# Gelu stages that scatter finished rows by their number instead of gathering them by slot, and a relu stage in one run of tiles

## The chip, the cores and the metric

The kernel runs on one core of a Trainium2 chip. The metric is the time on the device in microseconds (us); lower is better. The core's engines each follow a program of their own and meet at semaphores: TensorE (PE in the rows), VectorE (DVE), ScalarE (ACT), GpSimd (POOL) and SyncE (SP), which here only starts DMAs.

## The reference

2,048 tokens of 128 numbers go through six layers in float32:

```
x = x + 0.5 * FFN0(layernorm(x))   # stage a: 8 experts, gelu, top 2, width 512
x = x + attention(layernorm(x))    # b: 2 x 1,024 tokens, 16 heads, causal, rotated q and k
x = x + 0.5 * FFN0(layernorm(x))   # c: the same weights as a
x = x + 0.5 * FFN1(layernorm(x))   # d: 8 experts, relu, top 1, width 256
x = x + scan(layernorm(x))         # e: state-space scan
x = x + 0.5 * FFN1(layernorm(x))   # f: the same weights as d

FFN0: w, e = top_k(softmax(h @ Wr + br), 2)
      out  = sum over both: w * (gelu(h @ up[e].T) @ down[e].T)
FFN1: e    = argmax(h @ Wr + br), p its probability
      out  = p * (relu(h @ w1[e] + b1[e]) @ w2[e] + b2[e])
```

## The kernel before, in words

The tokens stay on chip in `x`, 16 tiles of 128 rows, as two blocks `b` of 8 tiles. A mixture sorts the rows of a block by expert, so that every tile of 128 sorted rows has one expert. In a gelu stage a block gives 16 row sets (8 tiles, two choices each) and at most NTG = 23 sorted tiles; in a relu stage 8 row sets and NTL = 15 tiles.

**A gelu stage** (a from 49.3 us, c from 570.3). For each block the tasks `stats`, `norm`, `turn` normalize and transpose the rows, `glogits`, `gpick`, `gcount`, `gslots` pick two experts and compute each row's slot (`gslot_of`). GpSimd then sends 16 indirect DMAs, each 128 rows of `xn` to the scratch memory `xs` (L1654, `gelu_scatter`); in stage a SyncE has cleared that memory with zeros first, and block 1's first scatter waits for it. SyncE loads the sorted rows to `gxt` in four pieces (GLOADS). Then come 46 tiles, block 0's and block 1's, as a software pipeline over 48 steps `s`: TensorE transposes tile s (L802), VectorE copies the expert's up weights (L1905; ScalarE does it from step HANDED = 34), TensorE multiplies tile s-1 (L811), ScalarE applies gelu to it (L1240), TensorE multiplies tile s-2 by the down weights (L820), and ScalarE copies the result into `gxt`. SyncE stores the finished tiles in four pieces to `ys`. When all four are there, GpSimd gathers them with 16 indirect DMAs of 128 rows (L1661, `gelu_gather`) to `gyg`, and the task `gadd` adds them to `x`, weight times row, in 16 operations on VectorE (L1835). The weights come from the task `gweights` at steps 16 and 17.

Between these, GpSimd also sends block 1's scatter (behind block 0's), in stage a a chain of small operations on the bias b2 (`bias_parts`, L1645) and the clearing of attention's padded areas (`clear_pads`). All in the order of its program: it has one queue, and so has SyncE.

**Other work beside the tiles.** Each engine holds a list `along` of tasks that it does behind its own part of a step. At HANDED, VectorE starts block 0's `gadd` and its normalization for the next stage, so that only block 1's remains for the next stage. In attention, block 1's tasks are called `second` and stand between the score blocks of the first unit: its `gadd` behind block 14.

**The first relu stage** (d, from 728 us). Block 0's slots are ready by then. Its tiles run in two runs: block 0's 15 (18 steps), then the list `between` (block 1's `gadd`, normalization, logits, slots), then block 1's scatter, load and tiles. A relu tile has a transpose (L863), up matmuls (L870), VectorE's copy (L1924), transposes back (L877), relu on ScalarE, down matmuls (L884, L886) and VectorE's copy of the result (L1934). Block 0's rows are stored, gathered and added in the second run. The last stage (f) has one run over both blocks already, and GpSimd writes each of its finished tiles to the output with one indirect DMA (L1711), rows by their token numbers, at the pace in which tiles end.

## Time and profile before

| | us |
|---|---|
| median of 3 runs | 1326.39 |
| lowest, highest | 1318.11, 1328.89 |
| profiled execution, device time | 1318.07 |
| its span in the trace | 1316.3 |

Shares of the span in which an engine is busy: PE 71%, DVE 54%, ACT 45%, POOL 45%. The mean granted clock of TensorE is 0.825 of full speed. In a row of windows stand the stretch, its length, the busy us and count of PE, PEld, DVE, ACT and POOL, the granted clock, the DMA share and GB/s. Every time in the rows counts from the start of the span. "Idle before" is the time for which an engine did nothing ahead of an instruction, and the name behind the arrow is what ended it; "remote" stands for a release that no instruction or DMA of the trace explains, "issue" for none at all.

### The profile page before, as it was taken

The page shows a single profiled execution, that of the slowest core. Times are in us where ns is not written, and L with a number is a line of the kernel's source. Part 1 is how long each engine was busy: PE and PEld are TensorE (multiplying, and loading weights), DVE is VectorE, ACT ScalarE, POOL GpSimd, SP SyncE. Part 2 cuts the span into 40 slices and gives each one's busy share as a digit, 9 for nine tenths or more (in the row PEclk, how much of TensorE's full clock was granted, in tenths as well). Part 3 has the DMA queues.
Part 4 walks back from the last instruction along what each step waited for, and adds up shares of the span by engine and source line. Part 5 has one row for each costly group of instructions (what it writes and reads, how often), then busy time and mean ns, then how long its engine had stood idle before and what let it go on. Part 6 is the DMA issues. An engine that isn't in the chain of part 4 may idle for free. (4 is left out here: it accounts for less than half of the span.)

```text
span 1316.3 us, 27353 instructions
## 1 busy us (share of the span) xinstructions
PE 940.3 (71%) x9756; PEld 616.6 (47%) x9756; DVE 714.2 (54%) x1903; ACT 595.3 (45%) x1264; POOL 586.3 (45%) x585
## 2 busy tenths in 40 slices
PE   2768763688888887775876655463788888886686
PEld 2668650212222223355765443223566666665464
DVE  4222247667778874322221152556578888886432
ACT  1224450246666667242454222256456566651243
POOL 2462325643333311414212427232468888883454
PEclk9969785669999998687979777786678999986688
DMA  6531112132211100031311211103311111101320
GB/s 221 159 98 47 33 46 49 32 93 63 63 33 33 31 3 1 22 121 49 95 30 47 73 37 55 43 4 132 80 34 38 39 39 40 39 24 65 117 87 16
DMA packets 113706, 76.72 MB, mean 58 GB/s; under 512 B 56768, under 2 KB 107980, under 8 KB 112616
## 3 DMA queue, kind: packets, MB, share of 16 engines
q1 hardware_dynamic: 106727, 61.32, 16.8%
q0 software_dynamic: 6848, 13.67, 3.4%
q8 instruction: 82, 1.34, 0.4%
q14 instruction: 49, 0.39, 0.1%
HBM read 41.98 MB, written 29.46 MB: 54 GB/s over the span
## 5 line engine op out<-in xcount | busy, mean ns | idle before, releaser
L1625 POOL TENSOR_TENSOR arena<-arena 128x512 f32<-128x512 f32 x126 | 215.0, 1725 | 86.6 <-ACT arena L1344 37.4
L1344 ACT ACTIVATE arena<-ps 128x512 f32<-128x512 f32 x256 | 143.4, 596 | 107.8 <-PE ps L1039 101.9
L1296 ACT ACTIVATE arena<-ps 128x1024 f32<-128x1024 f32 (+1 forms) x192 | 148.2, 810 | 86.8 <-PE ps L944 83.2
L2035 DVE TENSOR_TENSOR arena<-arena,ps 128x1024 f32<-128x1024 f32 x189 | 154.4, 857 | 18.7 <-PE ps L1052 17.7
L929 PE MATMUL ps<-arena 64*128 64x512 bf16 (+3 forms) x384 | 109.7, 363 | 57.0 <-DVE maxima L1963 20.8
L1963 DVE CUSTOM_DVE_ANT_0 arena<-ps,arena 128x512 f32<-128x512 f32 (+3 forms) x256 | 112.1, 488 | 46.8 <-PE ps L929 40.0
L811 PE MATMUL ps<-arena 128*128 128x128 f32 x736 | 106.6, 291 | 33.6 <-issue 21.4
L820 PE MATMUL ps<-arena 128*128 x736 | 106.0, 290 | 32.1 <-ACT arena L1240 20.1
L1549 POOL TENSOR_SCALAR_AFFINE_SELECT arena<-arena 128x512 f32<-128x512 f32 x64 | 41.1, 642 | 186.9 <-ACT arena L1296 186.4
L1905 DVE COPY arena<-arena 128x512 f32 x68 | 33.2, 489 | 163.1 <-PE ps L811 81.0
L811 PEld LDWEIGHTS ps<-arena 128*128 128x128 f32 x736 | 96.2, 204 | 39.9 <-issue 24.5
L1661 POOL DMA_INDIRECT arena<-ys_rows,gslot_of x64 | 61.4, 959 | 117.8 <-DMA ys_rows<-arena 99.3
L820 PEld LDWEIGHTS ps<-arena 128*128 128x128 f32 x736 | 96.3, 204 | 35.9 <-issue 35.7
L929 PEld LDWEIGHTS ps<-arena 64*128 64x128 bf16 x384 | 28.2, 95 | 179.6 <-DVE maxima L1963 90.0
L1654 POOL DMA_INDIRECT xs_rows<-xn,gslot_of x64 | 62.1, 971 | 90.0 <-DVE gslot_of L1822 57.6
L959 PE MATMUL ps<-arena 128*32 128x512 f32 (+3 forms) x768 | 89.0, 538 | 7.4 <-POOL arena L1549 7.4
L1966 DVE TENSOR_REDUCE maxima<-ps 128x1 f32<-128x512 f32 x128 | 81.0, 684 | 21.9 <-PE ps L929 20.5
L2047 DVE TENSOR_TENSOR arena<-arena 128x1024 f32<-128x1024 f32 x63 | 77.6, 1232 | 26.9 <-ACT arena L1344 26.9
L1067 PE MATMUL ps<-arena 128*32 128x128 f32 x2048 | 86.2, 321 | 0.1
L944 PE MATMUL ps<-arena 64*128 64x512 bf16 (+3 forms) x384 | 83.0, 352 | 4.4 <-ACT arena L1296 4.4
L1240 ACT ACTIVATE arena<-ps 128x512 f32<-128x512 f32 x92 | 55.2, 600 | 67.2 <-PE ps L811 35.2
L1052 PE MATMUL ps<-arena 12*128 12x128 bf16 x1024 | 56.6, 237 | 16.9 <-DVE arena L2035 14.1
(245 smaller groups left out, 1672.1 us busy)
## 6 DMA issues: line engine op xcount, KB each, us to landing
ys_rows<-arena SPq DMA_DIRECT2D x8, 512.0 KB, 3.5
xw_rows<-blank_dram SPq DMA_DIRECT2D x2, 1935.0 KB, 8.9
arena<-xs_rows SPq DMA_DIRECT2D x6, 512.0 KB
arena<-xw_rows SPq DMA_DIRECT2D x2, 1032.0 KB
xs_rows<-arena SPq DMA_DIRECT2D x4, 512.0 KB, 7.0
arena<-up_dram SPq DMA_DIRECT2D x4, 512.0 KB, 7.1
arena<-dn_dram SPq DMA_DIRECT2D x4, 512.0 KB, 7.8
arena<-up_dram SPq DMA_DIRECT2D x2, 1024.0 KB, 6.3
```

The lines of the kernel that those rows point to most:

```text
L811: mm = e.matmul(ps[:, n1 % 2, c * P:(c + 1) * P], gwup[:, n1 % 2, c * P:(c + 1) * P], gxT[:, n1 % 2, :], start=True, stop=True)
L820: mm = e.matmul(ps[:, 4 + n2 % 2, 0:P], ghT[:, n2 % 2, c * P:(c + 1) * P], wdn[:, bass.ds(ex, 1), c, :].rearrange("p e d -> p (e d)"), sta ...
L929: mm = e.matmul(ps[:, n % 2, m * w:(m + 1) * w], qT[vp][rows, i, h // HP, :], kT[v % 3][rows, 4 * half:4 * half + w // P, h // HP, :], sta ...
L944: mm = e.matmul(ps[:, 2 + 2 * pair + h, 0:w], kT[v % 3][rows, j, pair, :], qm[rows, vp, pair, half * 512 + q0:half * 512 + 512], start=Tru ...
L959: mm = e.matmul(ps[32 * h:32 * h + 32, 6 + half, q0:512], vpad[:, vp, j, h, :], probT[:, n % 2, h, 0:w], start=(j == 0), stop=(w == P), sk ...
L1067: mm = e.matmul(ps[32 * ml:32 * ml + 32, 6 + u % 2, 0:D], cz[:, u % 2, ml, (4 * mh + t4) * 32:(4 * mh + t4 + 1) * 32], hsf[t % 3][:, m * D ...
L1296: e.activation(probT[:, m % 2, 2 * pair:2 * pair + 2, 0:w], ps[:, 2 + 2 * pair:4 + 2 * pair, 0:w], ACT.Exp, scale=SCALE).then_inc(AT["exp_ ...
L1344: e.activation(to, ps[:, 4 + n % 2, :].rearrange("p (d m t) -> p t m d", d=DBK, t=TU), ACT.Exp, scale=-1.0).then_inc(SC["decay_ready"], 1)
L1625: e.tensor_tensor(hsf[t % 3][:, cols], decayf[u % 2][:, t4 * W + cols.start:t4 * W + cols.stop], hsf[(t - 1) % 3][:, cols], ALU.mult).then ...
L1963: ins = e.tensor_tensor_reduce(masked_s[n % 2][:, m * w:(m + 1) * w], of, causal[:, 4 * P - w:4 * P], 1.0, MASKED, ALU.add, ALU.max, to)
L1966: ins = e.tensor_reduce(to, of, AX.X, ALU.max)
L2035: e.tensor_tensor(to, to, of, ALU.add).then_inc(SC["added"], 1)
```

## The change

Scattering by row number in place of the gathers. The sorted row now has GRW = 130 numbers: 128 of data, its weight and the number of its place in the block's result, 2 x 1,024 rows. Both are put in ahead of the scatter, so `gweights` moves in front of `gcount` and `gslots`. The source of the scatter is a new area `gsrc` with one copy of the rows for each choice; ScalarE makes the second. The scatter's targets are cleared with a table `gblank` from memory whose rows carry a number out of bounds, which the later DMA drops. When a tile is finished, ScalarE copies it times its weight (a column of the tile), and GpSimd sends that tile at once, by the numbers in its rows, to `yk`. When all 23 of a block have landed, SyncE loads the result with one DMA to `gyg`, and `gadd` is two additions over 128x1024.

One run in the relu stage. `between` is gone; block 1's tasks hang on steps 0 to 7 of the tiles of block 0. GpSimd sends block 0's relu scatter behind tile AHEAD = 14 of the last gelu block. HANDED falls to 30, and in attention block 1's tasks start behind score block 3.

The core of the diff:

```diff
+GRW = D + 2
+AHEAD = 14
...
-HANDED = 34
+HANDED = 30
...
+        gsrc = [[at(a0, TOP * HT * GRW).rearrange("p (k i r) -> p k i r", k=TOP, r=GRW) for a0 in pair]
+                for pair in ((10240, 12320), (SIDE0, 6144))]
...
-        GROUTED = ["glogits", "gpick", "gcount", "gslots"]
+        GROUTED = ["glogits", "gpick", "gweights", "gcount", "gslots"]
...
-            scalar[16], vector[17] = weights, weights
...
-                between = [(gelus[1], "gadd", 1)] + rows_of(st, 1) + [t(w, 1) for w in ROUTED]
-                runs = ((0, NTL), (NTL, B * NTL))
-                along = {5: [t("rweights", 0)], NTL + 5: [t("rweights", 1)]}
+                along = {"vector": {0: [(gelus[1], "gadd", 1), t("stats", 2)], 1: [t("norm", 2), t("stats", 3)], 2: [t("norm", 3)],
+                                    5: [t("rpick", 1)], 7: [t("rslots", 1)]},
+                         "tensor": {2: [t("turn", 2)], 3: [t("turn", 3)], 4: [t("rlogits", 1)], 6: [t("rcount", 1)]},
+                         "scalar": {0: [t("stats", 2)], 2: [t("turn", 2), t("stats", 3)], 3: [t("turn", 3)]}}[engine]
+                along.update({9: [t("rweights", 0)], NTL + 5: [t("rweights", 1)]})
...
-            second = {14: (0, 1), 18: (2,), 19: (3, 4), 23: (5,), 24: (6,), 27: (7,)}
+            second = {3: (0, 1), 7: (2,), 8: (3, 4), 12: (5,), 13: (6,), 16: (7,)}
...
+            def clear(m, b):
+                sp.dma_start(scratch[f"xg{m}{b}"], t_in["gblank"]).then_inc(rows_clear[b], 16)
...
-            def gelu_put(m, b, stores):
-                for i0, i1 in stores:
-                    sp.wait_ge(GT["y_copied"], (B * m + b) * NTG + i1)
-                    sp.dma_start(scratch[f"ys{b}"][i0 * P:i1 * P, :].rearrange("(i p) d -> p i d", p=P), gxt[b][:, i0:i1, :]
-                                 ).then_inc(gys_in[b], 16)
-
+            def gelu_rows(m, b):
+                sp.wait_ge(gput[b], 16 * NTG * (m + 1))
+                sp.dma_start(gyg[b].rearrange("p k i d -> p (k i) d"),
+                             scratch[f"yk{b}"].rearrange("(n p) d -> p n d", p=P)).then_inc(ys_in[b], 16)
...
-                    put(0, STORES)
+                    put(0, STORES[:2])
                     fetch(1)
+                    put(0, STORES[2:])
...
+            elif what == "norm" and st["kind"] == 0:
+                b, tiles = g * TPB // HT, slice(g * TPB % HT, g * TPB % HT + TPB)
+                rows = gsrc[st["ghalf"] // B][b]
+                e.wait_ge(LN["xn_ready"], st["norm"] + g + 1)
+                e.copy(rows[:, 1, tiles, 0:D], rows[:, 0, tiles, 0:D]).then_inc(GT["rows_copied"], 1)
...
-                    e.copy(gxt[b][:, i, :], ps[:, 4 + n2 % 2, 0:P]).then_inc(GT["y_copied"], 1)
+                    row = gxt[b][:, i]
+                    e.activation(row[:, 0:D], ps[:, 4 + n2 % 2, 0:P], ACT.Copy, scale=row[:, D:D + 1]).then_inc(GT["y_copied"], 1)
...
             def gelu_scatter(m, b):
-                if m == 0:
-                    e.wait_ge(rows_clear[b], CLEAR)
+                e.wait_ge(rows_clear[b], CLEAR[m])
                 e.wait_ge(GT["slots_ready"], B * m + b + 1)
                 for k in range(TOP):
+                    if k == 1:
+                        e.wait_ge(GT["rows_copied"], NTB // B * (B * m + b + 1))
                     for i in range(HT):
-                        e.indirect_dma_start(scratch[f"xs{b}"], bass.IndirectOffsetOnAxis(ap=gslot_of[:, b, k, i:i + 1], axis=0),
-                                             xn[:, b * HT + i, :], None).then_inc(grows_moved[b], 16)
-
-            def gelu_gather(m, b):
-                e.wait_ge(gys_in[b], 16 * len(GSTORES) * (m + 1))
-                for k in range(TOP):
-                    for i in range(HT):
-                        e.indirect_dma_start(gyg[b][:, k, i, :], None, scratch[f"ys{b}"],
-                                             bass.IndirectOffsetOnAxis(ap=gslot_of[:, b, k, i:i + 1], axis=0)).then_inc(grows_moved[b], 16)
+                        e.indirect_dma_start(scratch[f"xg{m}{b}"], bass.IndirectOffsetOnAxis(ap=gslot_of[:, b, k, i:i + 1], axis=0),
+                                             gsrc[m][b][:, k, i, :], None).then_inc(grows_moved[b], 16)
+
+            def gelu_rows_out(m, b):
+                for i in range(NTG):
+                    if (m, b, i) == (1, 1, AHEAD):
+                        relu_scatter(relus[0], 0)
+                    row = gxt[b][:, i]
+                    e.wait_ge(GT["y_copied"], (B * m + b) * NTG + i + 1)
+                    e.indirect_dma_start(scratch[f"yk{b}"], bass.IndirectOffsetOnAxis(ap=row[:, D + 1:GRW].bitcast(U32), axis=0),
+                                         row[:, 0:D], None, bounds_check=TOP * S - 1, oob_is_err=False).then_inc(gput[b], 16)
...
-                gelu_gather(m, 0)
+                gelu_rows_out(m, 0)
                 if m == 0:
                     clear_pads()
-                    gelu_gather(0, 1)
+                gelu_rows_out(m, 1)
...
-                relu_scatter(st, 0)
-                if st is relus[0]:
-                    gelu_gather(1, 1)
-                    relu_gather(0, 0)
+                if st is relus[-1]:
+                    relu_scatter(st, 0)
                 relu_scatter(st, 1)
                 if st is relus[0]:
+                    relu_gather(0, 0)
...
+                    e.tensor_copy(rows.rearrange("p k i r -> p (k i) r")[:, :, D + 1:GRW].bitcast(I32), token_of[:].unsqueeze(2))
                     link(e.reciprocal(w[:, 0], w[:, 0]))
-                    link(e.tensor_scalar(w[:, 0], w[:, 0], 0.5, None, ALU.mult))
-                    link(e.tensor_tensor(w[:, 1], w[:, 0], gshift[:, g, :, E], ALU.mult))
+                    link(e.tensor_scalar(rows[:, 0, :, D], w[:, 0], 0.5, None, ALU.mult))
+                    link(e.tensor_tensor(rows[:, 1, :, D], rows[:, 0, :, D], gshift[:, g, :, E], ALU.mult))
                 elif what == "gadd":
-                    e.wait_ge(grows_moved[g], GMOVE * (2 * m + 2))
+                    e.wait_ge(ys_in[g], 16 * (m + 1))
+                    xs = x[:, g * HT:(g + 1) * HT, :]
                     for k in range(TOP):
-                        for i in range(HT):
-                            xs = x[:, g * HT + i, :]
-                            e.scalar_tensor_tensor(out=xs, in0=gyg[g][:, k, i, :], scalar=gweight[:, g, k, i:i + 1], in1=xs,
-                                                   op0=ALU.mult, op1=ALU.add).then_inc(GT["added"], 1)
-                        e.wait_ge(GT["added"], (q * TOP + k + 1) * HT)
+                        e.tensor_tensor(xs, xs, gyg[g][:, k], ALU.add).then_inc(GT["added"], 1)
+                        e.wait_ge(GT["added"], q * TOP + k + 1)
```

**GpSimd, from block 0's scatter of the second gelu stage to the end of the relu stage.** `xs`, `xg` are sorted rows, `ys`, `yk` results, the digit behind is the block (`xg10` is stage c, block 0). Before:

```order
L1654 DMA xs0_rows<-xn,gslot_of 2944x128 x16
L1654 DMA xs1_rows<-xn,gslot_of 2944x128 x16
L1661 DMA arena<-ys0_rows,gslot_of 128x128 x16
L1683 DMA xs0_rows<-xn,slot_of 2944x128 x8
L1661 DMA arena<-ys1_rows,gslot_of 128x128 x16
L1689 DMA arena<-ys0_rows,slot_of 128x128 x8
L1683 DMA xs1_rows<-xn,slot_of 2944x128 x8
L1701 MEMSET arena 128x4096
L1701 MEMSET arena 128x16384
L1689 DMA arena<-ys1_rows,slot_of 128x128 x8
```

Now:

```order
L1658 DMA xg10_rows<-arena,gslot_of 2944x130 x16
L1658 DMA xg11_rows<-arena,gslot_of 2944x130 x16
L1667 DMA yk0_rows<-arena 2048x128 x23
L1667 DMA yk1_rows<-arena 2048x128 x14
L1689 DMA xs0_rows<-xn,slot_of 1920x128 x8
L1667 DMA yk1_rows<-arena 2048x128 x9
L1689 DMA xs1_rows<-xn,slot_of 1920x128 x8
L1695 DMA arena<-ys0_rows,slot_of 128x128 x8
L1706 MEMSET arena 128x4096
L1706 MEMSET arena 128x16384
L1695 DMA arena<-ys1_rows,slot_of 128x128 x8
```

The two bursts of 16 gathers are gone and 46 scatters of finished tiles stand there, split behind the 14th of block 1; block 1's relu scatter is ahead of block 0's gather.

**VectorE, where block 1's rows enter the first relu stage.** Before, with the last three result copies of block 0's tiles ahead:

```order
L1934 COPY arena<-ps 128x128 x3
L1835 SCALAR_TENSOR_TENSOR x<-arena,gweight,x 128x128 x16
L1748 BN_STATS stats<-x 128x6 x4
L1753 BN_AGGR mv<-stats 128x2 x4
L1764 RECIPROCAL rstd<-std 128x4
L1771 TENSOR_SCALAR xn<-x,mv,rstd 128x128 x4
```

Now, with the first copies of block 0's tiles (L1924) between:

```order
L1863 CAST slot_of<-best8 128x8
L1839 TENSOR_TENSOR x<-x,arena 128x1024 x2
L1752 BN_STATS stats<-x 128x6 x4
L1757 BN_AGGR mv<-stats 128x2 x4
L1924 COPY arena<-ps 128x256
L1768 RECIPROCAL rstd<-std 128x4
L1775 TENSOR_SCALAR xn<-x,mv,rstd 128x128 x4
```

The 16 additions are two, and the norm of block 1 stands among the copies of block 0's first tiles instead of behind its last.

## Rows read from the trace of the kernel before

**Rows 1.** Windows of three stages.

```profile
49.30:186.00 136.70, 105.16 (x805) 98.97 (x804) 32.06 (x94) 63.77 (x163) 46.77 (x45) 0.86 0.28 79
570.30:710.60 140.30, 105.86 (x850) 100.36 (x848) 37.00 (x140) 70.61 (x171) 30.64 (x32) 0.88 0.21 66
728.00:837.70 109.70, 68.35 (x345) 47.80 (x342) 36.31 (x127) 33.39 (x100) 43.42 (x30) 0.77 0.16 46
```

**Rows 2.** Transposes L802 in five stretches: durations in ns, first and last start.

```profile
L802 PE MATMUL ps<-ident,arena x9: 272/273/273, 105.1 to 120.4; 128*128 128x128 f32 x9
L802 PE MATMUL ps<-ident,arena x5: 272/272/421, 122.3 to 146.8; 128*128 128x128 f32 x5
L802 PE MATMUL ps<-ident,arena x5: 273/273/421, 601.3 to 625.3; 128*128 128x128 f32 x5
L802 PE MATMUL ps<-ident,arena x4: 272/272/421, 648.0 to 670.5; 128*128 128x128 f32 x4
L802 PE MATMUL ps<-ident,arena x5: 272/401/421, 61.4 to 88.2; 128*128 128x128 f32 x5
```

**Rows 3.** Timelines of POOL and DVE, first gelu stage: start, duration, [idle before].

```profile
59.29 0.95 POOL L1654 DMA_INDIRECT xs_rows<-xn,gslot_of  x1 [13.95 <-DMA xs_rows<-arena]
120.36 1.02 POOL L1661 DMA_INDIRECT arena<-ys_rows,gslot_of  x1 [28.98 <-DMA ys_rows<-arena]
139.19 0.94 POOL L1661 DMA_INDIRECT arena<-ys_rows,gslot_of  x1 [0.31 <-issue]
121.74 0.43 DVE L1905 COPY arena<-arena 128x512 f32 x1 [1.47 <-PE ps L811]
```

**Rows 4.** Timeline of ACT, first gelu stage, same columns.

```profile
137.36 0.60 ACT L1240 ACTIVATE arena<-ps 128x512 f32<-128x512 f32 x1 [6.61 <-remote]
```

**Rows 5.** GpSimd's DMAs to the output, last stage (by line).

```profile
L1711 POOL DMA_INDIRECT out_dram<-arena x25: 981/982/993, 1255.7 to 1299.5; - x25
```

**Rows 6.** Timeline of DVE, last stage.

```profile
1254.50 0.35 DVE L1931 SCALAR_TENSOR_TENSOR arena<-ps,arena 128x128 f32<-128x128 f32 x1 [4.59 <-remote]
```

**Rows 7.** Timelines of DVE and POOL, first gelu stage.

```profile
82.08 3.00 DVE L1905 COPY arena<-arena 128x512 f32 x2 [12.23 <-remote]
101.78 0.22 DVE L1826 TENSOR_REDUCE gweight<-gshift 128x8 f32<-128x64 f32 x1 [2.22 <-ACT gshift L1207]
90.27 1.11 POOL L1645 CAST b2p<-arena 3x1024 bf16<-3x1024 f32 x1
```

**Rows 8.** Timelines of PE, DVE, POOL and ACT, opening of attention.

```profile
203.99 0.40 PE L929 MATMUL ps<-arena 64*128 64x128 bf16 x4 [16.96 <-issue]
217.29 4.41 DVE L1835 SCALAR_TENSOR_TENSOR x<-arena,gweight,x 128x128 f32<-128x128 f32 x16
243.38 4.49 POOL L1584 TENSOR_TENSOR arena<-arena,bqkv 128x2048 f32<-128x2048 f32 x1 [11.56 <-ACT arena L1317]
266.08 1.51 ACT L1296 ACTIVATE arena<-ps 128x768 f32<-128x768 f32 x2 [1.60 <-POOLq L1517]
268.42 1.94 PE L959 MATMUL ps<-arena 128*32 128x512 f32 x8 [2.95 <-POOL arena L1549]
```

**Rows 9.** The page, costliest groups and DMA issues (KB each, us to landing).

```profile
L2047 DVE TENSOR_TENSOR arena<-arena 128x1024 f32<-128x1024 f32 x63 | 77.6, 1232 | 26.9 <-ACT arena L1344 26.9
arena<-up_dram SPq DMA_DIRECT2D x2, 1024.0 KB, 6.3
```

**Rows 10.** Timelines of DVE, POOL and PE, first relu stage.

```profile
743.45 0.29 DVE L1934 COPY arena<-ps 128x128 f32<-128x128 f32 x1 [10.82 <-remote]
770.03 3.09 DVE L1835 SCALAR_TENSOR_TENSOR x<-arena,gweight,x 128x128 f32<-128x128 f32 x11
791.64 1.00 POOL L1683 DMA_INDIRECT xs_rows<-xn,slot_of  x1 [9.63 <-DVE slot_of L1860]
804.96 0.45 PE L863 MATMUL ps<-ident,arena 128*128 128x128 f32 x1 [13.13 <-issue]
```

**Rows 11.** Transposes L863 of the relu stage's second run (by line).

```profile
L863 PE MATMUL ps<-ident,arena x15: 272/273/472, 805.0 to 831.0; 128*128 128x128 f32 x15
```

More of the change, by code:

```diff
@@ L346, in gelu_tasks @@
             tensor, scalar, vector = {}, {}, {}
-            weights = [t("gweights", b) for b in range(B)]
             if st is gelus[0]:
@@ L379, in relu_tasks @@
                 before = [k for b in range(B) for k in rows_of(st, b) + [t(w, b) for w in ROUTED + ["rweights"]]]
-                between = []
-                runs = ((0, B * NTL),)
                 along = {}
-            return before, between, runs, along
+            return before, ((0, B * NTL),), along
         AT = {k: sem(f"att_{k}") for k in (
@@ L509, in _ @@
             sp.dma_start(before_f, t_in["before"]).then_inc(route_in, 16)
[L511 to L514 removed]
+            sp.dma_start(token_of[:], t_in["tokens"]).then_inc(route_in, 16)
+            def clear(m, b):
+                sp.dma_start(scratch[f"xg{m}{b}"], t_in["gblank"]).then_inc(rows_clear[b], 16)
             sp.dma_start(x[:, HT:NT, :], x_dram[:, HT:NT, :]).then_inc(x_in, 16)
[L517 to L518 removed]
+            clear(0, 0)
             for ex in range(0, E, 2):
@@ L561, in _ @@
                     sp.dma_start(scratch[f"xw{v - 3}"], t_in["blank"]).then_inc(rows_clear[v - 3], 16)
+                if v in (1, 2):
+                    clear(1, v - 1)
+                if v in (5, 6):
+                    sp.dma_start(scratch[f"xs{v - 5}"], t_in["blank"][0:NTL * P, 0:D]).then_inc(rows_clear[v - 5], 16)
                 sp.wait_ge(AT["unit_split"], 2 * v + 2)
@@ L692, in n_tile @@
                 return xw[:, i, 0:D]
+            if st["kind"] == 0:
+                return gsrc[st["ghalf"] // B][i // HT][:, 0, i % HT, 0:D]
             i0 = xn_at(st, i // TPB) + i % TPB * P
@@ L827, in relu_mixture_tensor @@
             nf = F1 // P
-            before, between, runs, along = relu_tasks(st, nxt)
+            before, runs, along = relu_tasks(st, nxt, "tensor")
             def keep(n):
@@ L843, in relu_mixture_tensor @@
             for first, last in runs:
-                if first > 0:
-                    for task in between:
-                        task_tensor(e, *task)
                 for s in range(first, last + 3):
@@ L855, in relu_mixture_tensor @@
                                 e.wait_ge(rows_moved[b], MOVE * (2 * m + 1))
-                            if st is relus[0]:
-                                keep(KEEP[1 + b])
+                            if st is relus[0] and b == 0:
+                                keep(KEEP[1])
                             e.wait_ge(RT["slots_ready"], st["half"] + b + 1)
@@ L1250, in relu_mixture_scalar @@
             nf = F1 // P
-            before, between, runs, along = relu_tasks(st, nxt)
+            before, runs, along = relu_tasks(st, nxt, "scalar")
             for task in before:
@@ L1254, in relu_mixture_scalar @@
             for first, last in runs:
-                if first > 0:
-                    for task in between:
-                        task_scalar(e, *task)
                 for s in range(first, last + 3):
@@ L1910, in relu_mixture_vector @@
             def relu_mixture_vector(e, st, nxt):
-                before, between, runs, along = relu_tasks(st, nxt)
+                before, runs, along = relu_tasks(st, nxt, "vector")
                 for task in before:
@@ L1914, in relu_mixture_vector @@
                 for first, last in runs:
-                    if first > 0:
-                        for task in between:
-                            task_vector(*task)
                     for s in range(first, last + 3):
@@ L2144, in constants @@
                                  np.full((NTL * P, 1), NOWHERE, np.int32).view(np.float32)], axis=1),
+        "gblank": np.concatenate([np.zeros((NTG * P, GRW - 1), np.float32),
+                                  np.full((NTG * P, 1), NOWHERE, np.int32).view(np.float32)], axis=1),
         "before": (n[:, None] < n[None, :]).astype(np.float32),
```

90 lines of the change are left out of this document (41 added, 49 removed).

## The prediction

> **What bounds the kernel now.** I read the windows by stage first, then the engines' timelines inside the four windows that the change touches. The chain of waits covers only the end, so it doesn't help here. In the gelu stages (49.3 to 186 and 570.3 to 710.6) no engine is full: TensorE's matmul records cover 105 of 137 us, its granted clock is 0.86 and 0.88 [rows 1]. Two paces explain that. Undisturbed, nine transposes L802, one a tile, start from 105.1 to 120.4: 15.3/8 = 1.91 us a tile. In four other places five starts, or four in the third, take 24.5, 24.0, 22.5 and 26.8 us, 6 to 7.5 a tile; the lowest are 6.1 and 6.0 [rows 2]. Each of the four lies on a burst in which GpSimd issues 16 indirect DMAs, one row set every (139.19-120.36)/15 = 1.26 us; the slow tiles go on until some 3 us after the last [rows 3]. What is late there is a signal: ScalarE stands for 6.61 us in which TensorE's matmuls were long over, with "remote" as releaser [rows 4]. So **a burst of indirect DMAs beside the tile pipeline costs its length plus 3 us, less the tiles that crawl through**.
>
> The counter-example matters most. In the last stage GpSimd issues one indirect DMA for each finished tile, 25 from 1255.7 to 1299.5, 43.8/24 = 1.83 us apart, and there the tiles run at pace [rows 5]: only the burst ahead of them left a 4.59 us remote wait at 1254.50 [rows 6]. The change turns the gelu gathers into that pattern. Its success depends on whether GpSimd is at pace, or behind and so in a burst.
>
> **The change, part by part.** The sums are against the profiled execution, 1318.07 us (span 1316.3), which is at the low end of the runs shown (1318.11 to 1328.89, median 1326.39).
>
> Opening. The weights now come ahead of the slots: five small VectorE operations of 0.22 us [rows 7], so +1.1 us in front of the first scatter. ScalarE's copy of the rows for the second choice lies beside TensorE's transposes: nothing, and 0.6 us for each at worst if that cover were gone. The blank rows are now copied from memory; they are issued where zeros went out before and have over 20 us: nothing. Rows of 520 instead of 512 bytes: nothing.
>
> First gelu stage (a). Block 1's scatter no longer waits for its clearing, which is issued earlier, so its burst moves from 59.29 to some 49, just when the tiles start. Before, it cost 26.8-4x1.91 = 19.2 us [rows 2, 3]. After: slow from 50.5 to 72, 21.5 us with 3.5 tiles, costs 14.8; behind it the eight chained operations on b2, which run to 91.4 before, lengthen weight copies (3.00 us for two) [rows 7] and cost perhaps 2.5. Term -1.9. The gather of block 0 goes: 24.5-7.6 = -16.9. The weights' stop at tile 16 goes (8x0.22 = 1.8 us of VectorE [rows 7], behind ScalarE's exponential, which I put at as much again with the restart): -3.
>
> Added: the y scatters. GpSimd reaches the first only after its b2 work, at some 82, with 9 tiles finished. It sends one every 1.26 us (0.796 a us), the crawling pipeline adds one every 6.1 (0.164), so the backlog drains in 9/0.63 = 14 us. With the 3 us behind it that is 17 us for 2.8 tiles: +12. From there on it's one scatter a tile, 1.26 in 1.91 us, and I take nothing: the bounds are 0 [rows 5] and the full crawl of 4.2 us a tile [rows 2]; I take the near end since the form is the same (one tile, rows of 512 bytes, indices beside them, out-of-bounds rows dropped). clear_pads between the blocks lets 3 tiles pile up: +3. Stage a: 1.1-1.9-16.9-3+12+3 = **-6**.
>
> Here a rule speaks against the change. VectorE's weight copy (0.43 us, 128x512 fp32, SBUF to SBUF) runs every tile; one of GpSimd's gathers was under way when the copy at 121.74 ran, another stood alone at 139.19, and the step stayed 1.26 us over all 16 [rows 3]. The Trainium skill (SBUF — State Buffer, "Who interferes with whom") says that such a copy locks GpSimd out of the shared port, so that its descriptors wait. By the rows the sum has no term; by the rule each scatter would be longer, which is rival 4.
>
> Attention's opening (186 to 268.4). It starts with an idle TensorE until 203.99, behind the two transposing DMAs and beside the second gather burst. Then come 16 additions of 4.41 us at 217.29, which now are two over 128x1024 each (such an operation takes 1.23 on average in another stage [rows 9]); and GpSimd's rotation from 243.38 on, for which ScalarE waits 1.60 us at 266.08 and TensorE 2.95 us at 268.42 [rows 8]. The gathers are gone (-4, a choice: their 3 us tail and some delay of the transposes), additions -2, and because block 1's tasks move from score block 14 to 3, the rotation starts earlier and the last two waits go, -4.5. Late next: block 1's y rows, landed and read back (1 MB takes 6.3 us [rows 9], so 1.3+3+6.3+1 = some 12 us after the last tile), while the score blocks start 15 to 18 us after it: covered by little, so I give 2.5 back. Term **-8**. SP's two clears ahead of transposes 1 and 2 have tens of us.
>
> Second gelu stage (c). The second gather goes: four starts from 648.0 to 670.5 are three steps, 22.5-3x1.91 = -16.8 [rows 2]. But block 1's scatter (601 to 620) stays, and GpSimd comes out of it with 15 finished tiles waiting: 15/0.63 = 24 us more of burst, in which 3.9 tiles pass: +16.4. Two copies and an earlier table change on ScalarE: +1.5. AHEAD: GpSimd stops at y tile 14 of block 1 for the relu slots (TensorE's count is at step 41), then sends 8 scatters and the 9 last tiles, 17x1.26 = 21 us of burst over the last 5 tiles, of which some two crawl fully: +9. The weights' stop -1. In return the relu stage starts sooner: 17.4 us lie between the last tile and 728 [rows 1]; after, the last y scatter, 3 us to land, SP's y load, then the tile load, 10.5 in all: -7. Sum -16.8+16.4+1.5+9-1-7 = **+2**.
>
> First relu stage (728 to 837.7). Now one run. Before: two runs with a seam: after the first, additions, norm, logits and slots up to 791.64, 8 scatters, tiles again at 804.96 [rows 10]. A tile takes (831.0-805.0)/14 = 1.86 us [rows 11], so 33 steps, the 30 tiles and 3 to fill and drain the pipeline, take 61.4. Block 1's scatter and block 0's gather become two bursts of 8 inside the run. At 743.45 a long burst ended in a remote wait of 10.82 [rows 10]; that of 8 in the last stage ended in one of 4.59 [rows 6], which with its restart I put at 6: 6 each. The routing tasks of block 1 sit between tiles; they fill VectorE's idle time where a tile leaves some, and hold the tiles where they wait in a chain: +8, between 0 and the 35 us that the seam takes (770.03 to 804.96). 61.4+12+8 = 81.4 against 109.7: -28. GpSimd's two memsets for the scan now end only about when the last y is stored: +2, a choice. Term **-26**.
>
> Sum: -6-8+2-26 = -38: 1318-38 = **1280 us**. The other runs shown lie up to 11 us above the profiled one, which I keep for the range.
>
> **The rivals.** (1) The y scatters don't crawl even when GpSimd is behind: rows 5 show a pace of 1.83, not 1.26, so nothing excludes it; against it, all four bursts did. Then 12+3+16.4+9 of the sum's costs go: **1240**. (2) Slower: even at one a tile they delay TensorE's signals. Place: steady gelu tiles, some 78 of 92; price 1.2 us a tile (0.6 on each of the two signals to ScalarE); -38+94 = +56, **1374**. It decides from 38/78 = 0.5 us a tile. For: a gelu tile has 17 matmuls where the last stage has 10, so more signals. Against: 25 in a row at pace [rows 5]. (3) The relu run buys little: VectorE in order stands through additions, norm and slots while the tiles wait, the tasks cost the whole 35 us instead of 8: 1280+27 = **1307**. (4) The lock: each scatter waits for a weight copy of 0.43, 1.69 us instead of 1.26; 9 tiles then drain in 9/(0.592-0.164) = 21 us and 15 in 35: +5 and +8 after the crawling tiles, and no room in the end phase, +4: **1297**; the rows of 0.95 us beside such copies speak against it.
>
> **How the numbers follow.** Forecast 0.55 (its own range 1262 to 1300), rival 1 0.18, rival 2 0.12, rival 3 0.10, rival 4 0.05. A change under 1% (13 us) can't be told from none. Faster: 0.53+0.18+0.05+0.03 = 0.79; same 0.02+0.05+0.02 = 0.09; slower 0.12. The range takes half of rival 1, which is at its lower end, and rival 3 with the 8 us by which the median lies above the profiled run: 1240 to 1315.
>
> **What would show it.** GpSimd's gather lines are gone and 92 scatters of y rows stand there, back to back from 82 to 96 and from 620 to 644, else one a tile; TensorE's transposes at 6 us in those stretches and at 1.9 outside. Stage a ends near 180, attention's first weighted sum starts near 254, relu's tiles start near 716 and end near 797. I'm wrong if the single scatters sit beside steps of over 2.4 us, if the 1.26 us bursts sit beside 1.9 us steps, if attention waits for the y rows, or if relu's first steps take over 5 us each.

## The result and the profile after

The changed kernel takes 1280.84 us (median of 4 runs, 1277.08 to 1286.18), the kernel before 1322.25 beside it; the ratio is 0.9696, 95% interval 0.9616 to 0.9776. The profiled execution took 1277.80 us, against 1318.07 before: 40.3 us less. The forecast was 1280.

From the page, the group of the y scatters (line, out<-in, count, busy us, mean ns, idle before and its releaser).

```profile
L1667 POOL DMA_INDIRECT yk_rows<-arena x92 | 91.5, 994 | 91.0 <-ACT arena L1250 75.1
```

Stage windows, with the columns of [rows 1]: stage a, stage c, the relu stage.

```profile
49.70:177.70 128.00, 101.40 (x807) 96.00 (x805) 39.99 (x95) 67.76 (x164) 76.39 (x74) 0.91 0.26 68
548.60:705.40 156.80, 103.94 (x850) 98.85 (x849) 34.37 (x125) 77.86 (x176) 67.51 (x69) 0.85 0.19 59
714.90:795.20 80.30, 61.49 (x333) 44.82 (x333) 32.45 (x115) 31.94 (x99) 32.51 (x18) 0.89 0.19 56
```

| from, to | before | after | difference | forecast |
|---|---|---|---|---|
| start to first tile of a | 49.3 | 49.7 | +0.4 | +1.1 |
| stage a, to its last down matmul | 136.2 | 126.9 | -9.3 | -7.1 |
| to the first weighted sum | 82.9 | 71.7 | -11.2 | -8 |
| attention, to the first tile of c | 301.9 | 300.3 | -1.6 | 0 |
| stage c, to its last down matmul | 139.7 | 155.7 | +16.0 | +9 |
| to the first relu tile | 18.0 | 10.6 | -7.4 | -7 |
| relu stage, to its last down matmul | 109.2 | 79.2 | -30.0 | -28 |
| the rest | 479.1 | 481.9 | +2.8 | +2 |

The marks are first starts of the transposes and of the weighted sums and last starts of the down matmuls in the two traces. The differences add up to -40.3. Stage c, whose gathers were taken away, is 16 us longer than before.

**What a burst does.** Transposes of the gelu tiles by stretches, as in [rows 2]:

```profile
L804 PE MATMUL ps<-ident,arena x5: 272/273/327, 49.7 to 56.0; 128*128 128x128 f32 x5
L804 PE MATMUL ps<-ident,arena x16: 272/273/273, 97.8 to 126.3; 128*128 128x128 f32 x16
```

GpSimd beside them (a timeline's start and duration; then groups by line with first and last start):

```profile
49.27 0.96 POOL L1658 DMA_INDIRECT xg_rows<-arena,gslot_of  x1 [3.58 <-DVE gslot_of L1826]
68.31 0.96 POOL L1658 DMA_INDIRECT xg_rows<-arena,gslot_of  x1 [0.30 <-issue]
L1667 POOL DMA_INDIRECT yk_rows<-arena x8: 982/984/1040, 82.2 to 91.3; - x8
L1667 POOL DMA_INDIRECT yk_rows<-arena x13: 982/982/984, 99.2 to 121.9; - x13
```

While the single y scatters follow the tiles, 12 steps of 1.89 us from 99.2 to 121.9, the tiles are at pace: 15 steps of 1.90. Beside block 1's scatter, 16 in (68.31-49.27)/15 = 1.27 us each, the first five tiles are at pace too, and then no transpose starts from 56.04 to 74.74. The trace before has the same: beside its burst from 59.29 on, transposes start at 61.35 and 63.25, at pace, and then at 71.87, 84.58 and 88.21. Over the whole stretch that looked like a slow crawl; it is tiles at pace, then a stop. The stop in the timelines of PE, ACT, SyncE and DVE (SPq is a DMA issue, here the loads that wait for the 16 scatters):

```profile
54.14 0.27 PE L804 MATMUL ps<-ident,arena 128*128 128x128 f32 x1
54.25 1.06 PE L813 MATMUL ps<-arena 128*128 128x128 f32 x8
56.04 0.27 PE L804 MATMUL ps<-ident,arena 128*128 128x128 f32 x1
61.52 0.37 ACT L1250 ACTIVATE arena<-ps,arena 128x128 f32<-128x128 f32 x1 [7.28 <-remote]
63.63 0.27 ACT L1230 COPY arena<-ps 128x128 f32<-128x128 f32 x1 [1.75 <-remote]
63.95 2.08 PE L813 MATMUL ps<-arena 128*128 128x128 f32 x8 [7.64 <-issue]
70.61 2.11 SPq L529 DMA_DIRECT2D arena<-xg_rows  x4
72.13 0.60 ACT L1244 ACTIVATE arena<-ps 128x512 f32<-128x512 f32 x1 [8.23 <-remote]
72.25 2.92 DVE L1908 COPY arena<-arena 128x512 f32 x2 [17.90 <-remote]
74.74 0.42 PE L804 MATMUL ps<-ident,arena 128*128 128x128 f32 x1
```

Counted in program order, the instructions pair up like this. The transpose of 54.14 is over at 54.41, and ScalarE's copy of it (L1230) starts at 63.63, 9.2 us later. The up matmuls of 54.25 are over at 55.31, and ScalarE's gelu (L1244) and VectorE's next weight copy, both of which wait for them, start at 72.13 and 72.25, 16.8 us later. In the other direction nothing is late: L1230 ends at 63.90, and TensorE's next up matmuls, which wait for it, start at 63.95. So it is TensorE's signals that arrive late, 9 us and then 17.

In stage c the backlog of 12 finished tiles joins the burst. Two stops stand there, until 598 and 619, as these rows of DVE and POOL show:

```profile
598.13 0.43 DVE L1908 COPY arena<-arena 128x512 f32 x1 [14.43 <-remote]
619.29 0.43 DVE L1908 COPY arena<-arena 128x512 f32 x1 [20.73 <-remote]
L1667 POOL DMA_INDIRECT yk_rows<-arena x12: 982/984/1027, 598.4 to 612.6; - x12
```

At the end of stage c the relu scatter of block 0 and seven finished tiles are a burst of 15 DMAs. The down matmuls that L1250 waits for at 695.53 are over at 684.68, the up matmuls that L1244 waits for at 701.86 at 687.25:

```profile
L1689 POOL DMA_INDIRECT xs_rows<-xn,slot_of x8: 955/959/962, 680.5 to 689.3; - x8
L1667 POOL DMA_INDIRECT yk_rows<-arena x7: 982/984/997, 690.6 to 698.3; - x7
695.53 0.37 ACT L1250 ACTIVATE arena<-ps,arena 128x128 f32<-128x128 f32 x1 [5.82 <-remote]
701.86 0.60 ACT L1244 ACTIVATE arena<-ps 128x512 f32<-128x512 f32 x1 [5.96 <-remote]
```

**Attention's opening** (against [rows 8]): TensorE starts at 191.26 instead of 203.99, the additions take 2.48 us instead of 4.41, the rotation starts at 219.71 instead of 243.38, and there is no wait in front of the first weighted sum.

```profile
191.26 0.40 PE L928 MATMUL ps<-arena 64*128 64x128 bf16 x4 [14.42 <-DMA arena<-arena]
248.33 1.93 PE L958 MATMUL ps<-arena 128*32 128x512 f32 x8
193.65 2.48 DVE L1839 TENSOR_TENSOR x<-x,arena 128x1024 f32<-128x1024 f32 x2
219.71 4.52 POOL L1586 TENSOR_TENSOR arena<-arena,bqkv 128x2048 f32<-128x2048 f32 x1 [13.45 <-ACT arena L1319]
```

**The relu stage** (against [rows 10, 11]): the first 12 steps, with block 1's tasks in them, take 29.1 us where 22.3 would be pace (1.86 a step); each burst of 8 stops the tiles once, 8.7 us and 11.7 us for two steps that take 3.7.

```profile
L862 PE MATMUL ps<-ident,arena x13: 272/273/446, 714.9 to 743.9; 128*128 128x128 f32 x13
L862 PE MATMUL ps<-ident,arena x3: 273/273/421, 743.9 to 752.6; 128*128 128x128 f32 x3
L862 PE MATMUL ps<-ident,arena x3: 272/421/421, 767.5 to 779.2; 128*128 128x128 f32 x3
L1689 POOL DMA_INDIRECT xs_rows<-xn,slot_of x8: 955/959/965, 738.8 to 747.6; - x8
L1695 POOL DMA_INDIRECT arena<-ys_rows,slot_of x8: 940/944/995, 763.1 to 771.9; - x8
```

### The profile page after: what moved, and what is told of

It is laid out like the page before. It is cut to its first block and busy times, and to the rows that moved or that the text cites. A ratio compares the mean times of both kernels' runs of the same rounds, so it can differ in the third digit from the quotient of the medians.

```text
span 1276.0 us, 27407 instructions
## 1 busy us (share of the span) xinstructions
PE 925.0 (72%) x9746; PEld 611.4 (48%) x9746; DVE 706.6 (55%) x1843; ACT 612.4 (48%) x1280; POOL 615.5 (48%) x612
## 5 line engine op out<-in xcount | busy, mean ns | idle before, releaser
L2035 DVE TENSOR_TENSOR arena<-arena,ps 128x1024 f32<-128x1024 f32 x189 | 154.9, 857 | 22.4 <-PE ps L1051 21.3
L928 PE MATMUL ps<-arena 64*128 64x512 bf16 (+3 forms) x384 | 107.6, 353 | 49.4 <-DVE maxima L1963 19.9
L1667 POOL DMA_INDIRECT yk_rows<-arena x92 | 91.5, 994 | 91.0 <-ACT arena L1250 75.1
L813 PE MATMUL ps<-arena 128*128 128x128 f32 x736 | 103.6, 286 | 40.3 <-ACT arena L1230 26.0
L822 PE MATMUL ps<-arena 128*128 x736 | 103.3, 286 | 37.8 <-ACT arena L1244 29.6
L813 PEld LDWEIGHTS ps<-arena 128*128 128x128 f32 x736 | 94.0, 200 | 45.5 <-ACT arena L1230 28.4
L822 PEld LDWEIGHTS ps<-arena 128*128 128x128 f32 x736 | 93.8, 200 | 40.8 <-issue 40.6
L1658 POOL DMA_INDIRECT xg_rows<-arena,gslot_of x64 | 62.5, 976 | 81.8 <-DVE gslot_of L1826 63.3
L943 PE MATMUL ps<-arena 64*128 64x512 bf16 (+3 forms) x384 | 80.3, 341 | 6.3 <-ACT arena L1298 6.3
L1244 ACT ACTIVATE arena<-ps 128x512 f32<-128x512 f32 x92 | 55.0, 598 | 58.5 <-remote 33.2
```

The costliest lines, as they stand in the source:

```text
L813: mm = e.matmul(ps[:, n1 % 2, c * P:(c + 1) * P], gwup[:, n1 % 2, c * P:(c + 1) * P], gxT[:, n1 % 2, :], start=True, stop=True)
L822: mm = e.matmul(ps[:, 4 + n2 % 2, 0:P], ghT[:, n2 % 2, c * P:(c + 1) * P], wdn[:, bass.ds(ex, 1), c, :].rearrange("p e d -> p (e d)"), sta ...
L928: mm = e.matmul(ps[:, n % 2, m * w:(m + 1) * w], qT[vp][rows, i, h // HP, :], kT[v % 3][rows, 4 * half:4 * half + w // P, h // HP, :], sta ...
L1667: e.indirect_dma_start(scratch[f"yk{b}"], bass.IndirectOffsetOnAxis(ap=row[:, D + 1:GRW].bitcast(U32), axis=0), row[:, 0:D], None, bounds_ ...
L2035: e.tensor_tensor(to, to, of, ALU.add).then_inc(SC["added"], 1)
```

## The experiments

The kernels ran in four jobs, each on a chip of its own, with the kernel before beside them: 1321.63, 1324.96, 1321.03 and, in the last, 1239.01 us. In the first three the kernel before takes what it took beside the changed kernel, so their times can be set against 1280.84 within a few us; the last stands apart and has its own paragraph.

**The relu stage in two runs again** (x1_two_runs):

```diff
-                along = {"vector": {0: [(gelus[1], "gadd", 1), t("stats", 2)], ...
+                between = [(gelus[1], "gadd", 1)] + rows_of(st, 1) + [t(w, 1) for w in ROUTED]
+                runs = ((0, NTL), (NTL, B * NTL))
...
-                    put(0, STORES[:2])
-                    fetch(1)
-                    put(0, STORES[2:])
+                    put(0, STORES)
+                    fetch(1)
...
+                    relu_gather(0, 0)
                 relu_scatter(st, 1)
```

> The changed kernel with its first relu stage in two runs again; the gelu stages are as changed. By the prediction's term the one run is worth 26 us, so 1281+26 = 1307 us. By rival 3 (the tasks of block 1 cost in the run what they cost at the seam) nothing or a few us: 1281 to 1286.

Measured: 1299.07 us, ratio 0.9827 (0.9800 to 0.9854). The one run is worth 18 us, not 26. Its transposes, by line:

```profile
L864 PE MATMUL ps<-ident,arena x30: 272/273/476, 721.8 to 813.0; 128*128 128x128 f32 x30
```

The stage takes 97.5 us from here to its last down matmul (819.3), against 79.2 with one run and 109.2 before. So 12 of the 30 us that this stage gained come from the rest of the change. Two reasons offer themselves, which no run separates: block 1's 16 gathers no longer stand beside its first run (the wait of 10.82 in [rows 10]), and the additions at the seam are two. Rival 3 falls.

**A rest between the indirect DMAs of block 1's scatter** (x2_spaced):

```diff
+            def rest(e):
+                pauses[0] += 1
+                e.memset(pause[:], 0.0).then_inc(paused, 1)
+                e.wait_ge(paused, pauses[0])
...
                                              gsrc[m][b][:, k, i, :], None).then_inc(grows_moved[b], 16)
+                        if b == 1:
+                            rest(e)
```

> After each indirect DMA of block 1's scatter in both gelu stages GpSimd clears 128x512 unused numbers (some 0.6 us), so they come some 1.9 us apart instead of 1.26. Theory A (a queue: TensorE's signals wait behind indirect DMAs that come faster than they are worked off): the stop of TensorE between 56.04 and 74.74 goes, its transposes stand 1.9 us apart beside these DMAs. Theory B (any indirect DMA issued beside the tiles holds up TensorE's signals, so a longer stretch of them costs more): the stop becomes 10 us longer. GpSimd comes to the finished tiles 10 us later by both, so the halts behind it grow: by A 1270 to 1285 us, by B 1295 to 1305.

Measured: 1285.22 us, ratio 0.9711 (0.9673 to 0.9749). Transposes and indirect DMAs, by line:

```profile
L807 PE MATMUL ps<-ident,arena x25: 272/273/273, 51.7 to 95.7; 128*128 128x128 f32 x25
L1666 POOL DMA_INDIRECT xg_rows<-arena,gslot_of x16: 953/963/966, 49.5 to 77.8; - x16
L807 PE MATMUL ps<-ident,arena x3: 273/421/421, 97.9 to 127.8; 128*128 128x128 f32 x3
L1677 POOL DMA_INDIRECT yk_rows<-arena x23: 982/983/1062, 92.5 to 121.0; - x23
```

With 1.89 us between the DMAs ((77.8-49.5)/15) 25 transposes stand 44.0/24 = 1.83 us apart: no stop. Theory A holds, and B falls. GpSimd then finds some 20 finished tiles and sends 23 back to back, and there the stop returns, 29.9 us for two steps: what the rests saved is lost there. A stop needs DMAs that come close together, and enough of them.

**How close, and what the new order waits for** (x5_all_spaced: the rest over 128x128 instead of 128x512, and `rest(e)` behind the y scatters as well):

> The changed kernel with a smaller rest (128x128 unused numbers cleared, some 0.3 us) behind each indirect DMA of block 1's scatter and behind each y scatter, so none of these come closer than some 1.55 us. Theory A (queue): if an indirect DMA is worked off within 1.5 us the halts of TensorE at 56 to 75, 87 to 95 and 585 to 622 go and the time falls to 1235 to 1250 us. If it takes longer, the halts come later in a stretch and last longer: 1275 to 1290. Theory B (any indirect DMA beside the tiles delays signals): the stretches of indirect DMAs are a quarter longer, 1285 to 1300.

Measured: 1287.19 us, ratio 0.9722 (0.9691 to 0.9753). Rows of PE, POOL and DVE:

```profile
L807 PE MATMUL ps<-ident,arena x8: 272/272/421, 56.1 to 78.1; 128*128 128x128 f32 x8
L1666 POOL DMA_INDIRECT xg_rows<-arena,gslot_of x16: 957/967/1042, 50.0 to 72.7; - x16
139.82 2.54 DVE L1850 TENSOR_TENSOR x<-x,arena 128x1024 f32<-128x1024 f32 x2 [27.63 <-DMA arena<-yk_rows]
```

At (72.7-50.0)/15 = 1.51 us a DMA seven steps take 22.0 us where 13.3 are pace, so 8.7 are lost, against 17.7 in the changed kernel (56.04 to 77.50 for two steps). The limit is thus between 1.5 and 1.9 us for one indirect DMA. Stage a as a whole gains nothing (127.4 us to its last down matmul, 126.9 in the changed kernel), and a new wait is why: the rest makes a y scatter take 2.0 us, more than a tile, GpSimd falls behind, and VectorE at step 30 stands 27.63 us for the rows of block 0; its norm is due at TensorE's step 36, whose transposes stop from 125.69 to 149.60.

**Bytes or rows.** x7_half_bytes sends half of each row, x9_half_rows half of the rows; in both, block 1's result is read from block 0's area, so their output is not the layer's:

```diff
# x7_half_bytes, block 1
-                        e.indirect_dma_start(scratch[f"xg{m}{b}"], ..., gsrc[m][b][:, k, i, :], None)
+                        e.indirect_dma_start(scratch[f"xg{m}{b}"].rearrange("n (h d) -> (n h) d", h=2), ..., gsrc[m][b][:, k, i, 0:GRW // 2], None)
# x9_half_rows, block 1
+                        half = slice(0, P // 2)
+                        e.indirect_dma_start(scratch[f"xg{m}{b}"], ... gslot_of[half, b, k, i:i + 1] ..., gsrc[m][b][half, k, i, :], None)
```

> Block 1's scatters in both gelu stages move 65 of a row's 130 numbers, for the same 128 rows (block 1's result is left out, and its y scatters drop rows). Theory A1 (the queue works off bytes): half the bytes, no halt between 56 and 75. Theory A2 (it works off rows or descriptors, whatever their size): the halt stays at some 17 us.

> Block 1's scatters in both gelu stages move 64 of the 128 rows of a tile, whole rows, still in 16 DMAs (half of block 1's rows are left out). With half the bytes per row the halt stayed at 18.5 us. Theory A2 (what is worked off slowly is a row or its descriptor): half the rows, the halt between 57 and 75 goes or is under 5 us. Theory A3 (it is the indirect DMA as such, whatever is in it): the halt stays at 16 to 19 us.

Measured, one run each: 1279.24 and 1280.63 us. The two transposes around the stop, of x7_half_bytes and then of x9_half_rows:

```profile
L804 PE MATMUL ps<-ident,arena x2: 273/347/421, 57.0 to 75.5; 128*128 128x128 f32 x2
```

```profile
L804 PE MATMUL ps<-ident,arena x2: 273/347/421, 57.8 to 75.7; 128*128 128x128 f32 x2
```

The stop is 18.5 and 17.9 us, against 18.7. Neither half the bytes nor half the rows shortens it. What is left is A3, the indirect DMA as such: how many there are and how close they come (1.27 us in x7_half_bytes, 1.20 in x9_half_rows).

**Block 0's relu scatter behind the last finished tile** (x4_no_ahead):

```diff
-                    if (m, b, i) == (1, 1, AHEAD):
-                        relu_scatter(relus[0], 0)
...
-                if st is relus[-1]:
-                    relu_scatter(st, 0)
+                relu_scatter(st, 0)
                 relu_scatter(st, 1)
```

> Block 0's relu scatter stands behind the last finished tile again instead of behind tile 14 of block 1. By the prediction's terms the halts at the end of stage c go (-9) and the relu stage starts later (+7): 1279. By the trace of the changed kernel the last tiles lose some 16 us beside that burst: the last down matmul ends near 690 instead of 704.7, the relu tiles start some 16 us behind it, near 707 instead of 714.9, 1273. Rival: the y scatters and the relu stage's beginning are late by the same, 1281.

Measured: 1273.41 us, ratio 0.9648 (0.9616 to 0.9681), 7 us better than the changed kernel by the medians. The intervals of the two ratios overlap, so the places in the traces have to show it.

```profile
L804 PE MATMUL ps<-ident,arena x46: 272/273/421, 551.5 to 685.6; 128*128 128x128 f32 x46
L862 PE MATMUL ps<-ident,arena x30: 272/273/421, 710.9 to 783.1; 128*128 128x128 f32 x30
```

The last down matmul of stage c starts at 690.3, 4.7 us behind the last transpose; in the changed kernel 21.7 lie between them (682.6 to 704.3). So AHEAD costs 17 us there and gives back 10 (20.6 instead of 10.6 from that matmul to the first relu tile): +7, which agrees with the medians, where the prediction had +9-7 = +2.

**The chain on b2 in the opening** (x8_b2_first, on top of x4_no_ahead; and x6_spaced_b2, which adds the rests of x5; SyncE's load of b2 moves up as well in both):

```diff
                 if m == 0:
+                    bias_parts()
                     gelu_scatter(0, 0)
                 gelu_scatter(m, 1)
-                if m == 0:
-                    bias_parts()
```

> x4_no_ahead with the chain on b2 in the opening, no rests. GpSimd reaches the finished tiles at 70 us instead of 82, in the halt, with 4 to 5 waiting instead of 9: the halt of 87 to 95 goes into the first, and the weight copies of 2.92 us beside the chain are 0.43. The prediction's terms for the backlog (12, at 9 tiles) and the chain (2.5) give 1273-8 = 1265. Rival: the backlog only joins the burst and lengthens the first halt by as much, 1273.

> As x5_all_spaced, with two more edits: GpSimd does the chain on b2 in the opening, where it is idle from 0.9 to 25.6, and block 0's relu scatter stands behind the last finished tile. Where 1.55 us is far enough: 7 us from the end of stage c (as x4_no_ahead) and some 5 us from stage a, so 1225 to 1240. Where it is not: 1262 to 1275.

Measured: 1273.99 us (ratio 0.9603, 0.9572 to 0.9634) and 1271.03 us (0.9579, 0.9535 to 0.9624). x8_b2_first misses its 1265: its median is that of x4_no_ahead, and its ratio is lower by 6 us' worth with intervals that overlap. VectorE's second group of normalizations and GpSimd's first scatter in it:

```profile
10.63 5.52 DVE L1772 TENSOR_SCALAR arena<-x,mv,rstd 128x128 f32<-128x128 f32 x4
30.30 1.16 POOL L1659 DMA_INDIRECT xg_rows<-arena,gslot_of  x1 [9.00 <-DVE gslot_of L1823]
```

The chain runs from 9.55 to 21.3 and the first scatter starts at 30.30; in x4_no_ahead it starts at 25.95, and the first tile at 51.2 instead of 54.5. Stage a itself is 3 us shorter (120.0 against 123.2 from first to last transpose), and the opening is 3 us longer. The traces show where: the four operations of L1772, which take 1.12 us in x4_no_ahead (from 10.67), take 5.52 beside the chain, and VectorE's last slots, for which GpSimd waits, are written at 29.22 instead of 24.86. So it is VectorE that GpSimd's chain delays. x6 has x5's wait for block 0's rows in it as well.

**Finished tiles before block 1's scatter in stage c** (x10_rows_first, on top of x4_no_ahead; x11_first_ahead is the same with AHEAD in place):

```diff
+                if m == 1:
+                    gelu_rows_out(m, 0, 0, FIRST)      # FIRST = 10
                 gelu_scatter(m, 1)
...
-                gelu_rows_out(m, 0)
+                gelu_rows_out(m, 0, FIRST * m)
```

> x4_no_ahead with GpSimd sending the first 10 finished tiles of stage c as they come, ahead of block 1's scatter, for whose slots it otherwise stands idle until 581. If the second halt of that stage (603.7 to 624.8 in x4_no_ahead) is the backlog of finished tiles joined to the burst of 16, it goes and the first one stays: 1273-19 = 1254 us. Rival: the halt depends only on how long GpSimd has work beside the tiles, the y scatters later in the stage stall TensorE instead: 1268 to 1273.

> x10_rows_first with AHEAD = 14 in place again (block 0's relu scatter behind tile 14 of block 1). If its loss in the changed kernel came from the backlog, here, with GpSimd at pace before it, only a burst of 8 is left: no difference to x10_rows_first within 5 us, or a gain of some 5. If it came from the burst itself beside the last tiles: 7 us slower than x10_rows_first, as the changed kernel is against x4_no_ahead.

Measured: x10_rows_first 1256.16 us, ratio 0.9528 (0.9470 to 0.9585), and x11_first_ahead 1267.47, ratio 0.9583 (0.9531 to 0.9635). x10_rows_first:

```profile
584.25 0.27 PE L805 MATMUL ps<-ident,arena 128*128 128x128 f32 x1
592.98 0.42 PE L805 MATMUL ps<-ident,arena 128*128 128x128 f32 x1
609.88 0.42 PE L805 MATMUL ps<-ident,arena 128*128 128x128 f32 x1
L805 PE MATMUL ps<-ident,arena x46: 272/273/421, 548.4 to 673.1; 128*128 128x128 f32 x46
L863 PE MATMUL ps<-ident,arena x30: 272/273/421, 698.0 to 767.1; 128*128 128x128 f32 x30
```

Stage c takes 124.7 us from first to last transpose, against 134.1 in x4_no_ahead: the two stops are 8.7 and 16.9 us (584.25 to 592.98 to 609.88) where x4_no_ahead has 16.6 and 21.1. The time is near the 1254 expected, but not in the way that was expected: the second stop did not go, both got shorter, and they gave 9 us of the 17. The rest of the difference lies in stretches that the edit leaves alone (3.1 us ahead of stage c, 3.1 in the relu stage) and can't be put down to it. This is the best version on chips with the same time before, 25 us below the changed kernel. With AHEAD in place x11_first_ahead is 11 us slower, on the same chip: from the first tile of c to the first of the relu stage it loses 5.7 us (155.3 against 149.6), near the 7 expected, and the rest again elsewhere. So it is the burst itself beside the last tiles, not the backlog ahead of it.

**Block 1's tasks in attention behind score block 14 again** (x3_second14):

```diff
-            second = {3: (0, 1), 7: (2,), 8: (3, 4), 12: (5,), 13: (6,), 16: (7,)}
+            second = {14: (0, 1), 18: (2,), 19: (3, 4), 23: (5,), 24: (6,), 27: (7,)}
```

> Only the tasks of block 1 in attention's opening start behind score block 14 again instead of 3. By the prediction the two waits of 1.60 and 2.95 us in front of the first weighted sum come back, 4.5 us less the 2.5 that an earlier wait for block 1's rows may cost now: 1281+2 to 1281+4.5. Rival: GpSimd's rotation is late either way, no difference.

Measured: 1289.0 us, ratio 0.9749 (0.9722 to 0.9776): 8 us slower, though only part of that is the edit's. From the last down matmul of stage a (181.9) to the first weighted sum (257.1) it takes 75.2 us, against 71.7 in the changed kernel and 70.9 in x1_two_runs, which has the opening unchanged: 3.5 to 4.3 us. Stage a itself, which the edit doesn't touch, is 5 us longer here, as in x1_two_runs (131.9 and 131.3 against 126.9): its stops differ by as much from run to run.

**The rest in stage c, on another chip** (x12_first_rest: x10_rows_first with the rest of x5 behind block 1's scatter in stage c alone):

```diff
+                        if (m, b) == (1, 1):
+                            rest(e)
```

> x10_rows_first with the rest of x5_all_spaced (128x128 unused numbers) behind each indirect DMA of block 1's scatter in stage c alone, so these come some 1.47 us apart. The two halts there (584 to 593 and 593 to 610 in x10_rows_first, 22 us lost) shrink to the 5 us that this distance cost in x5_all_spaced; but the tiles then finish beside it, some 12 wait when GpSimd comes to them, and their burst costs some 12 us (8 waiting cost 5 to 7 in stage a): 1256-22+5+12 = 1251 us. Rival: GpSimd, not the halts, sets the end of the stage, as it has its 4 us more of work: 1256 to 1260.

Measured: 1209.85 us, against 1239.01 before on that chip, ratio 0.9742 (0.9707 to 0.9776). The rows of stage a, which this kernel has as x4_no_ahead has it: transposes, block 1's scatter, y scatters; then a transpose of stage c.

```profile
L808 PE MATMUL ps<-ident,arena x33: 272/273/273, 57.5 to 118.2; 128*128 128x128 f32 x33
L1667 POOL DMA_INDIRECT xg_rows<-arena,gslot_of x16: 957/962/1163, 46.3 to 65.5; - x16
L1676 POOL DMA_INDIRECT yk_rows<-arena x23: 984/984/1234, 80.6 to 109.2; - x23
590.14 0.45 PE L808 MATMUL ps<-ident,arena 128*128 128x128 f32 x1 [9.53 <-issue]
```

The longest wait of x10_rows_first with a release that the trace doesn't explain (VectorE's weight copy; total us, times, longest):

```profile
DVE arena L1908 <- remote: 44.2, 4, 17.8
```

Here 33 transposes stand (118.2-57.5)/32 = 1.90 us apart, beside the second half of block 1's scatter at 1.28 us a DMA and beside 23 y scatters in 28.6 us, 1.30 each. There is no stop, and the list of waits of x12_first_rest has no remote release at all. Against x10_rows_first, stage a takes 105.3 us instead of 126.0 and the relu stage 68.0 instead of 75.3, while attention up to the first tile of c, with no burst beside tiles, takes 302.5 and 302.4. So in this job TensorE's signals are not late. The kernel before is 83 us shorter in it; the four places of [rows 2] lose 19.2+16.9+16.4+16.8 = 69 us, the two of [rows 6, 10] some 15 more, which is about that. The rest of x5 costs here: block 1's scatter in stage c runs until 586.3, SyncE's loads go out at 587.69, and the 24th tile, block 1's first, starts at 590.14, 11.6 us behind the 23rd. What the rest is worth where there are stops is not measured, nor is the changed kernel itself on this chip.

## Why the prediction was right, and where not

- **Total:** 1280 forecast, 1280.84 measured, and by the profiled executions -40.3 for -38. The forecast case held, and every part that was forecast to move by more than 2 us moved that way. That the total is so close is partly luck: stage c came out 7 us dearer, and stage a, the opening of attention, attention and the relu stage 2.2, 3.2, 1.6 and 2.0 us cheaper.
- **The pattern of rows 5:** right. One scatter for each tile at the tiles' pace costs nothing (99.2 to 121.9). Rival 2 falls.
- **A burst costs its length plus 3 us less the tiles that pass:** right in size for 16, wrong in how. The prediction let tiles crawl at 6.1 us each; they run at pace for the first 5 to 8 us of a burst and then stand. So short bursts cost less: the tiles waiting at 82 were given +12 and cost 7 (86.98 to 97.83 for two steps, 10.9-3.8). In stage c, 584.83 to 621.79 for two steps loses 33.2 where the trace before lost 17 in its burst (606.07 to 628.40); the prediction had +16.4 for that difference, and it is 16.2.
- **Rival 1** (y scatters don't stop the tiles) is true for the first few of a burst and false for the rest.
- **AHEAD** is the term that was mis-sized: "17x1.26 = 21 us of burst over the last 5 tiles, of which some two crawl fully: +9". It was +17 (x4_no_ahead), and those 8 us are what stage c came out above its +9. The way to the relu stage is 7.4 us shorter than before, for 7.
- **Opening of attention:** -11.2 for -8. The 2.5 us given back for a late read of block 1's rows weren't needed: the additions at 193.65 have no wait in front of them. x3_second14 prices the earlier tasks at 3.5 to 4.3, for 4.5.
- **Relu stage:** -30 for -28, but the prediction booked all of it to the one run. x1_two_runs gives that 18, and 12 to the rest of the change. The bursts of 8 cost 5.0 and 8.0 us, for 6 each, and block 1's tasks 6.8 (29.1-22.3), for 8.
- **The lock (rival 4):** the y scatters stand 1.30 us apart beside the weight copies (82.2 to 91.3), the gathers 1.26 [rows 3]. The rule of the Trainium skill (SBUF — State Buffer, "Who interferes with whom"), as the prediction read it, would have had the scatters wait for such copies; no run here shows that.

What isn't settled: what TensorE's signals wait in. Shown are the condition (more than four to six indirect DMAs in a row, closer than a limit between 1.5 and 1.9 us, in three of the four jobs and beside the changed kernel, whether rows are whole, halved or half as many) and the direction (TensorE's signals to ScalarE and VectorE, not those back).

## What to carry to other kernels

Before a scatter or gather is put beside a matmul pipeline, ask how many indirect DMAs come back to back, not how many bytes they move: one a tile was free here, and 16 in a row cost 17 us. If GpSimd stands idle before a burst, give it the work that would otherwise wait behind the burst (x10_rows_first: 9 us in its stage), and don't start the next stage's burst beside the last tiles of this one (6 to 7 us). And check a kernel tuned around such stops on a second chip: on the one where they were absent, a rest cost some 10 us of waiting for rows.

## What the runs showed of the hardware that was not expected

- The stops are there in some jobs and absent in another: the kernel before takes 1321 to 1325 us in three and 1239 in one, with the granted clock nearly the same (0.842 in x10_rows_first, 0.855 in x12_first_rest). Each job had a chip of its own, so the chip is the likely reason, but no run separates it from the time of the job.
- Halving the bytes or the rows of an indirect DMA left the stop at 18.5 and 17.9 us, and GpSimd spends 0.96 and 0.90 us on one, against 0.96.
- GpSimd's chain of small operations slows VectorE: four normalizing operations took 5.52 us beside it and 1.12 without it (x8_b2_first, x4_no_ahead).
- The stop doesn't end with the landing of the data: GpSimd is through with the last scatter at 69.27, SyncE, which waits for all 16 to land, issues its loads at 70.61, and TensorE's signals arrive at 72.13.
